# A graph network layer on one core: TensorE's step in the order z, n, edge work, with two of four edge tiles normalised on VectorE

## The reference: what is computed

```
h    = max(layernorm(x), 0)                                    # every row on its own, eps 1e-5
msg  = relu(concat(h[src], h[dst]) @ W1[type] + b1[type]) @ W2[type] + b2[type]
agg  = segment_sum(msg, dst, 100000)
gi   = agg @ W_ih.T + b_ih ; gh = h @ W_hh.T + b_hh            # three parts each: r, z, n
r    = sigmoid(i_r + h_r) ; z = sigmoid(i_z + h_z)
n    = tanh(i_n + r * h_n)
out  = x + (1 - z) * n + z * h
```

## Time and profile before

| | |
|---|---|
| median of 3 runs | 1842.27 us (1839.33 to 1843.18) |
| the profiled execution's own time | 1840.2 us |
| its span, first to last instruction | 1838.3 us |
| TensorE busy | 1667.1 us, 91% |
| VectorE busy | 1595.2 us, 87% |
| ScalarE busy | 1494.6 us, 81% |
| GpSimd busy | 1178.9 us, 64% |
| mean granted clock of TensorE | 0.995 of full speed |
| DMA, mean over the span | 174 GB/s |

### The profile page before, as it was taken

The page is one execution under the profiler, slowest core; times in us unless marked ns, Lnnn a source line. Parts: engine busy times, 40 slices in busy tenths (PEclk is TensorE's granted clock), DMA queues, the critical chain, the costliest instruction groups (busy, mean ns, idle before and its releaser), DMA issues.

```text
span 1838.3 us, 43100 instructions
## 1 busy us (share of the span) xinstructions
PE 1667.1 (91%) x10182; PEld 1416.6 (77%) x10182; DVE 1595.2 (87%) x4186; ACT 1494.6 (81%) x3401; POOL 1178.9 (64%) x1982
## 2 busy tenths in 40 slices
PE   0226799999999999999999999999999999999998
PEld 0125688888888888888888888888888888888787
DVE  8597798989888988898889888989899989898776
ACT  0025789889888898898888888889898889888795
POOL 5777777776776777777765656666666566666310
PEclk9999899999999999999999999999999999999999
DMA  2225677777777776777677777777777777777653
GB/s 70 51 48 139 168 195 194 192 192 192 198 187 193 191 194 186 187 192 191 187 193 187 190 188 187 187 190 189 189 190 188 190 186 192 189 187 191 161 136 100
DMA packets 477071, 319.72 MB, mean 174 GB/s; under 512 B 106705, under 2 KB 463009, under 8 KB 476962
## 3 DMA queue, kind: packets, MB, share of 16 engines
q10 hardware_dynamic: 261792, 156.12, 28.6%
q1 hardware_dynamic: 185730, 106.99, 25.3%
q0 software_dynamic: 29440, 55.47, 11.8%
HBM read 211.65 MB, written 106.72 MB: 173 GB/s over the span
## 4 chain that ended last, share of the span: by engine, by line
PE 73%; ACT 8%; issue 4%; ACTq 3%; DVE 2%; DMA 0%; SPq 0%; POOL 0%; DVEq 0%; POOLq 0%
PE bank L1329 16%; PE bank L1331 12%; PE bank L1330 12%; PE bank L1409 10%; PE bank L1399 5%; PE bank L1391 5%; PE bank L1421 3%; PE bank L1420 3%; PE bank L1437 3%; ACT n_h L1194 3%; PE bank L1447 3%; ACT n_zc L1282 2%; ACTq L1211 2%; ACT e_r L1270 2%; ACTq L1232 2%
## 5 line engine op out<-in xcount | busy, mean ns | idle before, releaser
L580 POOL DMA_INDIRECT e_x<-in_x,rows_now x816 | 799.6, 980 | 241.7 <-issue 233.4
L1177 ACT ACTIVATE e_h<-e_x,shift,rstd 128x128 f32<-128x128 f32 x816 | 355.3, 493 | 93.6 <-DVE shift L1048 93.6
L1194 ACT ACTIVATE n_h<-n_x,shift,rstd 128x128 f32<-128x128 f32 x784 | 362.8, 489 | 2.1 <-issue 2.1
L1329 PE MATMUL bank<-n_h_hi,whh_hi 128*128 128x512 f32 x588 | 263.0, 447 | 25.3 <-ACT n_zc L1282 18.3
L1113 DVE TENSOR_TENSOR n_d<-bank,n_n 128x512 f32<-128x512 f32 x196 | 135.5, 691 | 160.7 <-ACT n_n L1278 149.1
L1329 PE MATMUL bank<-n_a_hi,wih_hi 128*128 128x512 f32 x588 | 249.3, 424 | 0.9 <-DVE bank L1083 0.9
L1071 DVE TENSOR_SCALAR n_sel<-iota,n_rel 128x256 fp32r<-128x256 f32 x784 | 237.8, 365 | 8.6 <-POOL n_rel L631 7.2
L1409 PE MATMUL bank<-n_sel,n_win 128*128 128x256 f32 x1568 | 234.9, 292 | 8.6 <-DVE n_sel L1071 8.4
L1331 PE MATMUL bank<-n_h_hi,whh_lo 128*128 128x512 f32 x588 | 232.9, 396 | 0.0
L1330 PE MATMUL bank<-n_h_lo,whh_hi 128*128 128x512 f32 x588 | 232.7, 396 | 0.0
L1331 PE MATMUL bank<-n_a_hi,wih_lo 128*128 128x512 f32 x588 | 232.3, 395 | 0.0
(11 more groups left out here) (179 smaller groups left out, 3895.4 us busy)
## 6 DMA issues: line engine op xcount, KB each, us to landing
n_win<-messages SPq DMA_DIRECT2D x1568, 64.2 KB
messages<-e_msg ACTq DMA_DIRECT2D x204, 257.0 KB, 2.7
n_x<-in_x ACTq DMA_DIRECT2D x195, 256.0 KB
out<-n_out ACTq DMA_DIRECT2D x195, 256.0 KB
e_x<-in_x,rows_now POOLq DMA_INDIRECT x816
rows_now<-lists SPq DMA_DIRECT2D x204, 2.0 KB
lists<-picks,list_rows POOLq DMA_INDIRECT x72
w<-in_W SPq DMA_DIRECT2D x1, 512.0 KB, 4.5
```

The costliest lines, as they stand in the source:

```text
L580: G.indirect_dma_start(e_x[:, s, 2 * end + t, :], None, x, bass.IndirectOffsetOnAxis(ap=rows_now[:, s, t, end:end + 1], axis=0)).then_inc( ...
L1177: last = A.activation(e_h[:, s % 2, k, :], e_x[:, s, k, :], ACT.Relu, scale=rstd[:, slot, col + k:col + k + 1], bias=shift[:, slot, col + ...
L1194: last = A.activation(n_h[:, s % 2, cols], n_x[:, s, cols], ACT.Relu, scale=rstd[:, slot, col + 4 + k:col + 5 + k], bias=shift[:, slot, co ...
L1329: T.matmul(o, w_hi, v_hi, start=start, stop=False, skip_group_check=onto)
```

## The change

Four things are changed; the arithmetic stays the same.

1. TensorE's step becomes: r, hn, node transposes, aggregation, z, in, W1 products, back transposes, edge transposes, messages.
2. ScalarE's step is written to match: e_msg (of unit i-10, now at the head of the step), e_h 0 and 1, n_h 0, n_r, store of messages, n_h_hi, n_h 1, n_a_hi, store of out, load of x, n_h 2, n_zc, n_h 3, n_n, e_r, e_ht.
3. VectorE makes tiles 2 and 3 of e_h, as e_x * rstd + shift without Relu, behind n_sel (new function scale_edges), and counts them in a new semaphore e_scaled. TensorE's edge transposes and GpSimd's gathers and its last operation for rstd wait for e_scaled as well as e_normed.
4. The Relu of those tiles is taken in the copy out of PSUM: e_ht = Relu(BE0) in place of Copy. For tiles 0 and 1, which ScalarE makes with Relu as before, it changes nothing.

The diff, cut to the new function, to ScalarE's head of the step and copy of e_ht, and to what follows the aggregation on TensorE:

```diff
+            def scale_edges(i, m):
+                q, s, third = i - 7, (m - 7) % UNROLL, (m - 7) % 4
+                if not within(q, UNITS):
+                    return
+                dve.wait_ge(ln_shifted, q - third + 4)
+                if due(q - 1):
+                    dve.wait_ge(e_turned, q - 1)
+                for k in (2, 3):
+                    col = 8 * third + k
+                    last = V.tensor_scalar(e_h[:, s % 2, k, :], e_x[:, s, k, :], rstd[:, s // 4, col:col + 1],
+                                           shift[:, s // 4, col:col + 1], ALU.mult, ALU.add)
+                last.then_inc(e_scaled, 1)
...
             def step(i, m):
-                normalise_edges(i, m, (0, 1, 2))
+                q, s = i - 10, (m - 10) % UNROLL
...
+                    A.activation(e_msg[:, s, :, 0:D], bank[BE1][:, message_part].rearrange("p (t d) -> p t d", t=2),
+                                 ACT.Copy).then_inc(e_high, 1)
+                normalise_edges(i, m, (0, 1))
+                normalise_nodes(i, m, (0,))
...
-                    A.activation(e_ht[:, s, :], bank[BE0][:], ACT.Copy).then_inc(e_evaced, 1)
...
+                    A.activation(e_ht[:, s, :], bank[BE0][:], ACT.Relu).then_inc(e_evaced, 1)
...
+                    pe.wait_ge(n_red, g + 1)
+                    gate(BRZ, 1, s, "ha").then_inc(n_gate_z, 1)
+                    pe.wait_ge(n_ted, g + 1)
+                    gate(BIN, 2, s, "a", onto=True).then_inc(n_gate_in, 1)
```

More of the change, by code:

```diff
@@ L364, in gnn_layer @@
         e_normed = sem("e_normed")
+        e_scaled = sem("e_scaled")
         e_turned = sem("e_turned")
@@ L655, in inverse_roots @@
                     pool.wait_ge(e_normed, first - 4)
+                    pool.wait_ge(e_scaled, first - 4)
                 if due(first - LAG + 5):
@@ L671, in step @@
                         pool.wait_ge(e_normed, i - 7)
+                        pool.wait_ge(e_scaled, i - 7)
                 if h is not None:
@@ L1173, in normalise_edges @@
                 slot, col = wait_norm(i, m)
-                if 0 in tiles and due(q - 1):
+                if due(q - 1):
                     act.wait_ge(e_turned, q - 1)
@@ L1254, in step @@
                     if due(g - 1):
-                        act.wait_ge(n_gate_z, g - 1)
+                        act.wait_ge(n_gate_in, g - 1)
                     A.activation(n_h_hi[:, s, :], bank[BT[s]][:], ACT.Copy).then_inc(n_hhi, 1)
+                normalise_nodes(i, m, (1,))
+                if within(g, NG):
                     act.wait_ge(n_summed, g + 1)
                     A.activation(n_a_hi[:, s, :], bank[BA][:], ACT.Copy).then_inc(n_ahi, 1)
-                normalise_nodes(i, m, (0,))
                 store_out(i, m)
                 load_x(i, m)
+                normalise_nodes(i, m, (2,))
+                g, s = i - LAG, (m - LAG) % 2
+                if within(g, NG):
+                    act.wait_ge(n_gate_z, g + 1)
+                    if due(g - 1):
+                        act.wait_ge(n_eed, g - 1)
+                    A.activation(n_zc[:, s, :], bank[BRZ][:], ACT.Sigmoid, bias=bneg[:, 1:2],
+                                 scale=-1.0).then_inc(n_zed, 1)
+                normalise_nodes(i, m, (3,))
+                if within(g, NG):
+                    act.wait_ge(n_gate_in, g + 1)
+                    if due(g - 1):
+                        act.wait_ge(n_ded, g - 1)
+                    A.activation(n_n[:, s, :], bank[BIN][:], ACT.Tanh, bias=bih[:, 2:3]).then_inc(n_ned, 1)
                 q, s = i - 9, (m - 9) % 2
@@ L1384, in step @@
                     gate(BHN, 2, s, "h").then_inc(n_gate_hn, 1)
-                q, s = i - 8, (m - 8) % 2
-                if within(q, UNITS):
-                    pe.wait_ge(e_normed, q + 1)
-                    if due(q):
-                        pe.wait_ge(e_evaced, q)
-                    for k in range(4):
-                        last = T.transpose(bank[BE0][:, k * P:(k + 1) * P], e_h[:, s, k, :], ident[:])
-                    last.then_inc(e_turned, 1)
                 g, s = i - LAG + 1, (m - LAG + 1) % 2
@@ L1422, in step @@
                     last.then_inc(e_hid, 1)
-                g, s = i - LAG, (m - LAG) % 2
+                g, s = i - LAG - 1, (m - LAG - 1) % 2
                 if within(g, NG):
-                    pe.wait_ge(n_ted, g + 1)
-                    gate(BIN, 2, s, "a", onto=True).then_inc(n_gate_in, 1)
-                    pe.wait_ge(n_red, g + 1)
-                    gate(BRZ, 1, s, "ha").then_inc(n_gate_z, 1)
+                    pe.wait_ge(n_eed, g + 1)
+                    if within(g + 1, NG):
+                        pe.wait_ge(n_ted, g + 2)
+                    elif due(g):
+                        pe.wait_ge(n_outed, g)
+                    for k in range(TILES):
+                        last = T.transpose(bank[BHN][:, k * P:(k + 1) * P], n_e[:, s, k * P:(k + 1) * P], ident[:])
+                    last.then_inc(n_back, 1)
+                q, s = i - 8, (m - 8) % 2
+                if within(q, UNITS):
+                    pe.wait_ge(e_normed, q + 1)
+                    pe.wait_ge(e_scaled, q + 1)
+                    if due(q):
+                        pe.wait_ge(e_evaced, q)
+                    for k in range(4):
+                        last = T.transpose(bank[BE0][:, k * P:(k + 1) * P], e_h[:, s, k, :], ident[:])
+                    last.then_inc(e_turned, 1)
                 q, s = i - 9, (m - 9) % 2
@@ L1438, in step @@
                     last.then_inc(e_messaged, 1)
-                g, s = i - LAG - 1, (m - LAG - 1) % 2
-                if within(g, NG):
-                    pe.wait_ge(n_eed, g + 1)
-                    if within(g + 1, NG):
-                        pe.wait_ge(n_ted, g + 2)
-                    elif due(g):
-                        pe.wait_ge(n_outed, g)
-                    for k in range(TILES):
-                        last = T.transpose(bank[BHN][:, k * P:(k + 1) * P], n_e[:, s, k * P:(k + 1) * P], ident[:])
-                    last.then_inc(n_back, 1)
                 if isinstance(i, int) and i == CHECK_STEP:
```

37 lines of the change are left out of this document (11 added, 26 removed).

## The result

The changed kernel took 1903.69 us (median of 4 runs, 1902.92 to 1904.15) against 1842.19 us (4 runs, 1839.33 to 1843.18) on the same chip: ratio 1.0336, 95% interval 1.0318 to 1.0354. It is 61.5 us slower. The forecast was 1862 us with a range up to 1888: the sign was right, the size was a third of what came. The profiled execution took 1903.6 us, its span 1901.7 us (before: 1840.2 and 1838.3). The clock plays no part: in 600 to 1700 us the granted clock was 1.00 in both traces.

A forecast was written before the change was run, and what follows sets the result against it. A ring between TensorE and ScalarE was taken as the bound; its new arcs, 3.82 + 3.76 + 0.76 = 8.34 us against 8.25, gave 1840.2 + 17 + 3 + 2 = 1862 us, range 1826 to 1888.

The forecast's parts named there:

- What bounds the kernel before: Loop step of 8.25 us: a closed ring of TensorE and ScalarE, 4.25 + 3.85 + 0.15 us, with two DMA issues on ScalarE.
- A: Rival: e_r comes in time, TensorE becomes the bound at 8.03 us a step, 1782 us in all; chance 0.09.
- First arc: TensorE, r start to n_a_hi start: edge transposes leave this stretch, 4.25 - 0.43 = 3.82 us.
- Second arc: ScalarE, n_a_hi to the end of e_r, with both DMA issues: 3.76 us (3.69 to 3.83) against 3.85 before.
- VectorE's tiles: Two e_h tiles behind n_sel: 0.32 us a step, barely covered by idle time; +3 us in about ten early steps.
- the ring through VectorE: Check from n_n through n_d and n_e to n_sel: n_sel done 2.25 us after r, wanted at 2.60, 0.35 us of room.
- Rival D: VectorE takes the ring over: n_sel late for the aggregation, 0.25 us over in every step, 1910 us; chance 0.08.
- Third arc: New stretch, e_r through the message product on TensorE to the next r: 0.76 us, ends 0.60 and 0.83.
- B: Rival, a little faster: the ring closes near its short end, 8.11 to 8.23 us a step, about 1830 us; chance 0.16.
- ScalarE's relief: ScalarE 0.84 us lighter a step, about 170 us busy time in all, without a gain since it then waits for the aggregation.
- The edges: Early steps where nothing covers VectorE's two tiles, +3 us; last steps without edge work, n_n ending ScalarE's row, +2 us.
- GpSimd at no cost: GpSimd's turn also waits for e_scaled, about 2.6 us after r against 2.74 before, so begins no later: cost 0.

The follow-up runs named there:

- the fastest version of the new order: The changed kernel with all four e_h tiles on ScalarE ahead of n_r and the load of x at the end of ScalarE's step: 1795.5 us.

## Why the prediction was wrong

*What bounds the kernel before.* Right. The two issues on ScalarE's arc were what held the step above TensorE's own: taking one of them off gave 8.07 us a step and 1784.5 us, next to the 8.03 and the 1782 worked out for the ring open. It opened by another hand than A's, since no activation behind an issue started while it ran.

*First arc.* Right: 3.77 us against 3.82, and with the edge transposes gone ScalarE no longer waits for the aggregation (5 waits, 10.8 us, against 195 and 68.4).

*Second arc: the step that failed.* "The two issues are moved with nothing to cover them. If they take as long, the next activation starts 1.31 us after n_a_hi." They did not take as long: it started 1.62 us after n_a_hi in the step read, where the forecast took 1.24. The second issue is an instruction with a wait of its own, for VectorE's n_xh, and I priced it by its length only, though the built program shows the wait (`L1228 ISA [waits n_xhed]`). The forecast's own count, carried on with distances of the trace after, gives the ring: n_d at 7.13 us, n_xh's start 5.21 us behind n_d (before 4.71, and 0.52 for the tiles), 0.68 for n_xh, 0.17 and 0.45 to n_h, 1.36 to n_n; with n_n at 6.40 the ring closes at 7.13 + 5.21 + 0.68 + 0.17 + 0.45 + 1.36 - 6.40 = 8.60 us, where the step was 8.57. All but the tiles' 0.52 and the hand-over of 0.17 could have been had, within some 0.1 us, from the trace before. The Trainium skill says, in "DMA: Bandwidth & Descriptors", section "Anatomy of one DMA", on GpSimd's path, that a DMA's semaphore wait happens on the issuing sequencer before dispatch. ScalarE's issues behave so here: n_h stood 139 times, 145.0 us in all, behind the issue that waited for n_xh.

*VectorE's tiles: the term that was mis-sized.* 0.32 us forecast, from four instructions of 0.16 that compare with one scalar; measured 0.52 from the first tile's start to the statistics. "In a full step this is covered, barely" was false. The check of the ring through VectorE stopped at n_sel and the aggregation (rightly: that wait came 2 times), and never asked for what stands behind the tiles. Counted this way, the wait with the tiles at 0.32 gives a ring of 8.40 against the forecast's 8.34, and the 0.20 more for the tiles make it 8.60. Without the wait the longer tiles would have moved nothing in that sum, so it took both errors to lose 0.26 us a step.

*Rival D.* VectorE did take the ring over, and its price of 1910 is near, by luck: the condition I gave, n_sel late for the aggregation, occurred 2 times, and the 0.25 us a step that I priced were those of another wait.

*Third arc.* 0.63 us against 0.76, next to its short end of 0.60; e_r last of ScalarE's ring and TensorE waiting for it, as forecast. With the first arc that makes the forecast step 0.18 us too long: its +0.09 for the order is -0.09, and the run of the order alone measured 8.30 against 8.36. So B, a little faster, was the truer forecast for the order by itself.

*ScalarE's relief.* 156 us less, and none of it on the path, as forecast. VectorE's busy time rose by 94 us where 65 were named.

*The edges.* Startup: 6.0 us instead of 3. The new order with ScalarE's tiles is 2.6 us behind at the first node step, the old order with VectorE's tiles 6.6. The tail: 62.0 us behind seven node steps before the last, 63.4 at the end, so 1.4 us where 2 were forecast.

*GpSimd at no cost.* True only because the step was long. Its turn did begin later: VectorE's tiles were done 2.84 us after r in the step read (1122.33 - 1119.49), not 2.6, and the turn waited 204.3 us for VectorE's tiles, 123.0 for ScalarE's before. As soon as the steps were at 8.03 us this decided: most of the 26 us in the old order, 27 between early and late tiles in the new.

What stays open: why the fastest version of the new order (1795.5 us) is still 11 us above the old order's 1784.5. Only 0.3 us of it is startup; by the last node step it is 9.8. I have not taken it apart. Nor did a run take away the wait alone and leave both issues in their place, as one more n_x buffer would: that the wait costs what it does rests on the runs with VectorE's tiles added and taken away under the same two issues (8.36 to 8.67 in the old order, 8.30, 8.42 and 8.68 in the new).

## What to carry to other kernels

A DMA issue on a computing engine is an instruction like any other: when it is moved, write down its length and its semaphore, and ask what stands behind it. A profile names the instruction that sat idle, not the one whose wait held it, so an activation that waits for something it doesn't read points to what stands ahead of it. Put such an issue where the engine's next work is not on the ring, and check every consumer of a moved result, also those (a gate, a buffer's next load) that are on no engine's critical path yet.

## What the runs showed of the hardware

- An activation behind a DMA issue starts 0.05 to 0.17 us after the issue ends (1125.83 to 1125.88 and 1124.83 to 1124.88 in the new order, 1129.81 to 1129.98 in the old), in none of these steps during it. In the kernel before, none of the 189 e_r behind the load's issue started less than 0.10 us after its end. The sequencer itself runs ahead: in the kernel before with the load last, the issue at 1129.38 us comes in the program behind e_msg, which started only at 1129.65. So the one issue behind two queued activations cost nothing here, while the second of two in a row cost 0.41 us behind the same activations (e_r at 1.31 us against 0.90).
- VectorE's scale and add with two scalars for each partition takes 0.26 us for 128x128 (start to start), against 0.16 us for the compare of the earlier trace rows.
- An instruction that only issues a DMA can be what holds an engine though the profile shows it short: the load's issue is 0.40 us long in the timeline, and its wait for n_xh appears as idle time of the activation behind it.
- In the changed kernel four n_sel took 1.13 to 1.15 us in 124 steps of 196 and 1.27 us or more in 53, as at 1111.88 us (1.28 us), where two e_h tiles, too, took 0.68 instead of 0.60. GpSimd's small operations for the root ran beside 45 of the 53 and beside none of the 124; beside 47 of the 124 ran gathers or fetches of the pick lists. But with VectorE's tiles late, 183 steps with gathers alone beside them were long. What the cause is was not tried.
